# Expert results of a gated transformer block: scattered to DRAM by token instead of stored by sorted tile and gathered

## The reference

```
logits = x_flat @ Wr                       # 2048 x 8
w, ind = top_k(logits, 2); w = softmax(w)
for each expert e:                         # hidden 1024 in layer 1, 512 in layer 2
    y_e = gelu(x_flat @ W1e + b1e) @ W2e + b2e
    acc += combine[:, e] * y_e             # combine is zero for an expert the token does not use
x = x + tanh(g) * acc                      # layer 2 adds its own normalised input as well
```

## Time and profile before

| | us |
|---|---|
| median of three runs | 1596.48 |
| span of the profiled execution, first to last instruction | 1607.0 |
| PE / DVE / ACT / POOL busy in the span | 1331.3 / 965.3 / 864.4 / 706.4 |
| last matmul of the last tile, layer 1 | ends at 818.3 |
| first attention matmul of layer 2 (L940) | 898.97 |
| last matmul of the last tile, layer 2 | ends at 1252.0 |
| first attention matmul of layer 3 | 1330.62 |

### The profile page before, as it was taken

How to read it: one execution, slowest core, us unless ns; L and a number is a source line. 1 busy time by engine, 2 the same in 40 slices (tenths; PEclk the granted TensorE clock), 3 DMA queues, 4 the chain that set the end, 5 groups by cost and what they waited for, 6 DMA issues and landing times.

```text
span 1607.0 us, 29299 instructions
## 1 busy us (share of the span) xinstructions
PE 1331.3 (83%) x9524; PEld 954.1 (59%) x9524; DVE 965.3 (60%) x2636; ACT 864.4 (54%) x1718; POOL 706.4 (44%) x823
## 2 busy tenths in 40 slices
PE   1699899987987499999986699838989767995985
PEld 1355489754655399999963456527868434555433
DVE  6779653427866633333345588574535467867787
ACT  2356854335885255555523388535545245885564
POOL 4557330125623477676045473157772536623000
PEclk9989999997999699999998699968999987997998
DMA  9989030279921334633145985024643479920001
GB/s 286 294 128 143 4 115 1 82 215 173 131 37 60 123 93 140 200 143 109 46 138 170 209 122 82 2 89 146 202 154 113 149 216 177 129 43 1 0 14 40
DMA packets 144175, 189.63 MB, mean 118 GB/s; under 512 B 21936, under 2 KB 110384, under 8 KB 143984
## 3 DMA queue, kind: packets, MB, share of 16 engines
q0 software_dynamic: 79264, 103.35, 32.7%
q1 hardware_dynamic: 64768, 84.41, 16.3%
HBM read 128.96 MB, written 50.99 MB: 112 GB/s over the span
## 4 chain that ended last, share of the span: by engine, by line
PE 51%; DVE 14%; POOL 11%; DMA 10%; issue 6%; ACT 6%; another core or an unknown queue 1%; SPq 0%; DVEq 0%; POOLq 0%; ACTq 0%
PE PS L1176 8%; PE PS L1156 8%; PE PS L997 6%; PE PS L940 5%; DMA stack<-mt 3%; PE PS L967 3%; DVE nm L2052 2%; PE PS L1034 2%; PE PS L1168 2%; DMA qk_parts<-q_parts 2%; POOL weights L747 2%; DMA wslot<-ys_sorted,pos 2%; POOL weights L742 1%; PE PS L977 1%
## 5 line engine op out<-in xcount | busy, mean ns | idle before, releaser
L2052 DVE TENSOR_REDUCE nm<-PS 128x2 f32<-128x512 f32 x384 | 251.7, 680 | 50.4 <-PE PS L940 50.3
L1176 PE MATMUL PS<-weights,hh 128*128 x936 | 188.9, 291 | 3.2 <-DVE hl L2365 3.2
L1156 PE MATMUL PS<-weights,xh 128*128 x468 | 171.6, 422 | 10.2 <-DVE xl L2349 4.6
L940 PE MATMUL PS<-stack 48*128 48x256 f32 x1024 | 142.1, 359 | 41.6 <-DVE nm L2052 12.9
L645 POOL DMA_DIRECT2D stack<-mt x128 | 71.5, 559 | 223.7 <-ACT mt L1485 220.8
L1476 ACT ACTIVATE probs<-PS 128x512 f32<-128x512 f32 x256 | 138.9, 595 | 45.7 <-PE PS L967 22.3
L940 PEld LDWEIGHTS PS<-stack 48*128 48x128 f32 x1024 | 85.6, 206 | 125.8 <-issue 65.0
L1476 ACT ACTIVATE xng<-PS 128x512 f32<-128x512 f32 x256 | 138.9, 594 | 39.8 <-PE PS L977 21.6
L1176 PEld LDWEIGHTS PS<-weights,hh 128*128 128x128 f32 x936 | 152.0, 192 | 4.6 <-issue 4.3
L1643 ACT ACTIVATE hh<-PS 128x512 fp32r<-128x512 f32 x117 | 65.6, 596 | 131.2 <-PE PS L1168 127.9
L1176 PE MATMUL PS<-weights,hl 128*128 x468 | 132.7, 284 | 0.0
(11 more groups left out here) (321 smaller groups left out, 3102.4 us busy)
## 6 DMA issues: line engine op xcount, KB each, us to landing
stack<-qk_parts POOLq DMA_DIRECT2D x128, 256.0 KB, 4.1
qk_parts<-stack SPq DMA_DIRECT2D x32, 512.0 KB
qk_parts<-q_parts SPq DMA_DIRECT2D x32, 512.0 KB, 8.0
stack<-qk_parts POOLq DMA_DIRECT2D x128, 128.0 KB, 3.7
weights<-W_dram POOLq DMA_DIRECT2D x12, 1024.0 KB, 8.1
ys_sorted<-yo SPq DMA_DIRECT2D x78, 128.0 KB
wide<-ctxT_dram SPq DMA_DIRECT2D x16, 512.0 KB, 5.9
weights<-W_dram POOLq DMA_DIRECT2D x12, 512.0 KB, 5.3
```

Of the source, the lines that this page charges most:

```text
L940: mm = pe.matmul(PS[:, (2 * t + h) % 3, qt * S:(qt + 1) * S], q[rows, qt * P:(qt + 1) * P], kk[rows], start=True, stop=True)
L1156: add = lambda x, w: pe.matmul(PS[:, hid_bank(p) + h, :], x[:, p, c, :], w, start=False, stop=True, skip_group_check=True)
L1176: add = lambda x, w: pe.matmul(o, x, w, start=False, stop=True, skip_group_check=True)
L2052: nc.vector.tensor_reduce(nm[:, j % 2, at:at + 2], PS[:, (2 * t + h) % 3, :].rearrange("p (q n) -> p q n", q=2), AX.X, ALU.max, negate=Tru ...
```

## The change

Results stay in SBUF: `result(i)` is the place in `wide` (i < 16) or the `home` of tile i, which the gathered tile has left by then. POOL, after its last weight split, issues 39 indirect scatters, tile by tile, each behind `yo_done` of that tile, to a DRAM tensor `yt` laid out by expert choice and token; padding rows go to rows of their own at its end. The index table `into` is made in `plan` beside `idx`, by six DVE operations where two stood (`rows_of_tiles`, called for 8 and for 31 tiles). SP loses its 39 stores; after the last `load_tile` it loads the projections, then the context once the first 16 scatters have landed, then, once all have, the results by eight plain loads of 512 KB. DVE adds four blocks for one choice, four for the other, then does four statistics.

```diff
+        def result(i):
+            return wide[:, i * D:(i + 1) * D] if i < 2 * AHEAD else home(i)
...
-        ys = nc.dram_tensor("ys_sorted", (NT * P, D), F32, kind="Internal").ap()
+        yt = nc.dram_tensor("y_tokens", (P + 2 * T + NT * P, D), F32, kind="Internal").ap()
...  # SP
-                sp.wait_ge(y_done[2], 24)
+                sp.wait_ge(y_done[2], 16)
...
-                    sp.dma_start(ys[2 * T:], io["ctx"][0:NT * P - 2 * T, :]).then_inc(later_in, 16)
+                    sp.dma_start(xt[0:P], io["ctx"][0:P, :]).then_inc(later_in, 16)
...
-                    def store_tile(i, p):
-                        sp.wait_ge(yo_done, n0 + i + 1)
-                        sp.dma_start(ys[P * i:P * (i + 1), :], yo[:, p]).then_inc(ys_out[p], 16)
-                    for i in range(AHEAD - 3):
-                        store_tile(i, i % 2)
                     for i in range(AHEAD, NT):
...
                         load_tile(i, i % 2)
-                        if 0 <= i - 2 * AHEAD - 2 < GROUPS:
-                            load_ctx(i - 2 * AHEAD - 2)
-                        store_tile(i - 3, (i - 3) % 2)
                     load_proj(l + 1)
-                    for i in range(NT - 3, NT):
-                        store_tile(i, i % 2)
+                    sp.wait_ge(yt_out[0], 16 * l * 2 * AHEAD)
+                    for g in range(GROUPS):
+                        load_ctx(g)
+                    sp.wait_ge(yt_out[1], 16 * l * (NT - 2 * AHEAD))
+                    for g in range(GROUPS):
+                        for m in range(2):
+                            first = P + m * T + g * 512
+                            sp.dma_start(yg[:, m * TILES + 4 * g:m * TILES + 4 * g + 4, :],
+                                         yt[first:first + 512, :].rearrange("(t p) d -> p t d", p=P)).then_inc(yg_in[2 * g + m], 16)
...  # POOL
-                    pool.wait_ge(placed, l)
-                    for p in range(2):
-                        pool.wait_ge(ys_out[p], 16 * ((NT + 1 - p) // 2) * l)
-                    for k in range(FED[l]):
-                        if k >= 8:
-                            pool.wait_ge(y_done[l], added(k - 8))
-                        nc.gpsimd.indirect_dma_start(yg[:, k, :], None, ys,
-                                                     bass.IndirectOffsetOnAxis(pos[:, k % 2, k // 2:k // 2 + 1], 0)
-                                                     ).then_inc(yg_in[k % 8], 16)
+                    pool.wait_ge(placed, 2 * l)
+                    for i in range(NT):
+                        pool.wait_ge(yo_done, NT * (l - 1) + i + 1)
+                        nc.gpsimd.indirect_dma_start(yt, bass.IndirectOffsetOnAxis(into[:, i:i + 1], 0), result(i), None
+                                                     ).then_inc(yt_out[i // (2 * AHEAD) > 0], 16)
...  # PE
-                pe.wait_ge(idx_done, 2 * l)
+                pe.wait_ge(placed, 2 * l)
...  # DVE
+            def rows_of_tiles(l, k, first, part, block):
+                n = part.shape[1]
+                at = slice(first, first + n)
+                tmp = lambda r: scan[:, 0].rearrange("p t e -> p (t e)")[:, 32 * (r + 1):32 * (r + 1) + n]
+                ts, tt = nc.vector.tensor_scalar, nc.vector.tensor_tensor
+                ts(tmp(0), block, TILES + 0.5, -float(T), ALU.is_gt, ALU.mult).then_inc(route_v[l], 1)
+                dve.wait_ge(route_v[l], k + 1)
+                tt(tmp(1), part, tmp(0), ALU.add).then_inc(route_v[l], 1)
+                dve.wait_ge(route_v[l], k + 2)
+                nc.vector.scalar_tensor_tensor(idx[:, at], block, float(P), tmp(1), ALU.mult, ALU.add).then_inc(idx_done, 1)
+                nc.vector.scalar_tensor_tensor(tmp(2), block, 0.5, pad_row[:, at], ALU.is_lt, ALU.mult).then_inc(route_v[l], 1)
+                dve.wait_ge(route_v[l], k + 3)
+                tt(tmp(0), part, tmp(2), ALU.add).then_inc(route_v[l], 1)
+                dve.wait_ge(route_v[l], k + 4)
+                nc.vector.scalar_tensor_tensor(into[:, at], block, float(P), tmp(0), ALU.mult, ALU.add).then_inc(placed, 1)
+                return k + 4
...
-                nc.vector.tensor_copy(pos[:], posf[:]).then_inc(placed, 1)
...
-                    nc.vector.tensor_copy(yo[:, p], PS[:, 5, 0:D]).then_inc(yo_done, 1)
+                    nc.vector.tensor_copy(result(i), PS[:, 5, 0:D]).then_inc(yo_done, 1)
...
+                for g in range(GROUPS):
+                    for m in range(2):
+                        dve.wait_ge(yg_in[2 * g + m], 16 * l)
+                        for t in range(4):
+                            at = 4 * g + t
+                            if m:
+                                dve.wait_ge(y_done[l], 8 * g + t + 1)
+                            nc.vector.scalar_tensor_tensor(x_res[:, at, :], yg[:, m * TILES + at, :], gt[:, 6 + m, at:at + 1],
+                                                           x_res[:, at, :], ALU.mult, ALU.add).then_inc(y_done[l], 1)
+                    for t in range(4):
+                        dve.wait_ge(y_done[l], 8 * g + t + 5)
+                        stats(2 * l + 2, 4 * g + t)
+                    group_variances(2 * l + 2, g)
```

More of the change, by code:

```diff
@@ L68 @@
 ROUTE = 17
-PLANNED = 56
+PLANNED = 59
 BY_GROUP = (0, 4, 6)
@@ L226, in build @@
         idx = sb("idx", [P, NT], U32, fs)
+        into = sb("into", [P, NT], U32, fs)
         late = sb("late", [P, NT - 4 * AHEAD, D], F32, fs)
@@ L297, in ctx_at @@
             return xnT[:, :, g * 512:(g + 1) * 512]
-        xt = nc.dram_tensor("x_tokens", (T, D), F32, kind="Internal").ap()
-        ys = nc.dram_tensor("ys_sorted", (NT * P, D), F32, kind="Internal").ap()
+        xt = nc.dram_tensor("x_tokens", (P + T, D), F32, kind="Internal").ap()
+        yt = nc.dram_tensor("y_tokens", (P + 2 * T + NT * P, D), F32, kind="Internal").ap()
         parts = nc.dram_tensor("qk_parts", (2, 2, 2 * DH, PAIRS, T), F32, kind="Internal").ap()
@@ L2238, in plan @@
                     dve.wait_ge(later_in, 64)
+                    ts(pad_row[:], iotas[:, 2 * TILES + 1:2 * TILES + 1 + NT], float(P), col("part"), ALU.mult, ALU.add)
                 for m in range(2):
@@ L2294, in plan @@
                 dve.wait_ge(idx_mm, 2 * l - 1)
-                then(nc.vector.tensor_copy(late[:, 0, 0:AHEAD], PS[:, 6, 0:AHEAD]))
-                nc.vector.scalar_tensor_tensor(idx[:, 0:AHEAD], PS[:, 6, AHEAD:2 * AHEAD], float(P), late[:, 0, 0:AHEAD],
-                                               ALU.mult, ALU.add).then_inc(idx_done, 1)
+                k = rows_of_tiles(l, k, 0, PS[:, 6, 0:AHEAD], PS[:, 6, AHEAD:2 * AHEAD])
                 for e in range(8):
@@ L2329, in plan_late @@
                     ins = tt(ids_late[:, at, rest:], ids_late[:, at, 0:rest],
-                             iotas[:, 0:TILES].unsqueeze(2).broadcast_to([P, TILES, rest]), ALU.mult)
+                             iotas[:, 1 + m * TILES:1 + (m + 1) * TILES].unsqueeze(2).broadcast_to([P, TILES, rest]), ALU.mult)
                 then(ins)
@@ L2333, in plan_late @@
                 dve.wait_ge(idx_mm, 2 * l)
-                then(nc.vector.tensor_copy(late[:, 0, 0:rest], PS[:, 7, 0:rest]))
-                nc.vector.scalar_tensor_tensor(idx[:, AHEAD:], PS[:, 7, rest:2 * rest], float(P), late[:, 0, 0:rest],
-                                               ALU.mult, ALU.add).then_inc(idx_done, 1)
+                rows_of_tiles(l, k, AHEAD, PS[:, 7, 0:rest], PS[:, 7, rest:2 * rest])
             def sparse(l):
@@ L2367, in d, with e @@
                                                 ).then_inc(hl_done, 1)
-                def e(i, p, turn):
+                def e(i):
                     dve.wait_ge(tiles_done, t0 + i + 1)
-                    before = ((NT + 1) // 2 if p == 0 else NT // 2) * (l - 1) + turn - 1
-                    if not (isinstance(turn, int) and before == 0):
-                        dve.wait_ge(ys_out[p], 16 * before)
-                    nc.vector.tensor_copy(yo[:, p], PS[:, 5, 0:D]).then_inc(yo_done, 1)
+                    nc.vector.tensor_copy(result(i), PS[:, 5, 0:D]).then_inc(yo_done, 1)
                 dve.wait_ge(tables, l)
@@ L2395, in sparse @@
                     dve.wait_ge(ln_x, 1)
[L2396 to L2401, removed]
-                        nc.vector.scalar_tensor_tensor(x_res[:, at, :], yg[:, k, :], gt[:, 6 + n // 2, at:at + 1], x_res[:, at, :],
-                                                       ALU.mult, ALU.add).then_inc(y_done[l], 1)
-                    if t % 4:
-                        g = t // 4
-                        stats(2 * l + 2, t - 2)
-                        stats(2 * l + 2, t - 1)
-                        dve.wait_ge(y_done[l], 2 * t + 4)
-                        stats(2 * l + 2, t)
-                        stats(2 * l + 2, t + 1)
-                        group_variances(2 * l + 2, g)
-                        if g + 1 < GROUPS:
-                            keys_low(l + 1, g + 1)
-                        else:
```

(9 more changed lines are left out.)

13 lines of the change are left out of this document (5 added, 8 removed).

## The result

Before and after were timed in turn on one chip: 1641.59 us after (median of 4 runs, 1640.85 to 1645.09) against 1597.53 us before (1594.42 to 1599.38). The ratio is 1.026, with a 95% interval of 1.022 to 1.030. **The change makes the kernel 44 us slower; 7 us faster was forecast, and the time lies above the range.** The profiled execution has a span of 1639.0 us against 1607.0, with PE busy 1334.7 us at a mean clock of 0.916.

What follows compares the result with a forecast made beforehand. PE bounds layer 1's tiles; the winnable part lies between tiles and attention. Loads -14.2 and -2.6, plan +2.0 give -14.8; plus 8 for hand-offs absent in the runs, -7: 1596.48 to 1589 us, range 1579 to 1604.

Steps and rivals of the forecast that it cites:

- Tile loop: Both layers' tiles: stores leave SP, scatters go to idle POOL; caught up by about 802, 17 us late in layer 2.
- rival C: Layer 2's scatters cost more than gathers, 1.6 us each, ending 13.7 us later: 1603 us; chance 0.20.
- turns of layer 1 grow beyond 6.73 us while scatters run: Sign against the forecast: PE's tiles in layer 1, following at 6.73 us, slow down beside POOL's scatters.
- Scatter price, 1.25 us: POOL's scatters behind its last split: each taken to cost 1.25 us, like gathers in a run.
- Late hand-offs "absent in the runs": DVE and ACT waits after indirect DMA runs, 18 us in the profile: 10.5 us of them taken as absent when timed.
- The 10.5 us between its profile and its median: Profiled span 1607.0 us against run median 1596.48: the profiled execution held at least 10.5 us that the runs don't.
- Loads, layer 1: Between tiles and attention, eight plain loads replace gathers: low part of first queries at 860.5, 14.2 us earlier.
- 828.3 + 32 + 2 = 862.3: Layer 1 terms: first load there at 828.3, four groups of work 32 us, 2 us lost to a late key store.
- Loads, layer 2: Between tiles and attention, plain loads wait for the last scatter: low part of first queries at 1310.5, 2.6 us earlier.
- Plan, +2.0 us: Index plan, both layers: more small DVE operations delay first gather and second tile, +1.0 us a layer; bounds 0 and +4.
- The 8 us taken off: Share of the 14 us of late hand-offs between tiles and attention assumed absent in the runs, so not winnable.
- POOL's tail of 17 us: Layer 2: 39 scatters at 1.253 us from 1220.1 end at 1269.0, 17 us after the last tile.

Runs made afterwards that it cites:

- e1: The changed kernel without any scatter, its eight loads reading x_tokens instead: 1587.34 us, ratio 0.991 to the kernel before.
- e3: The changed kernel with each scatter replaced by a plain DMA of the same tile from the same queue: 1570.63 us, ratio 0.980 to the kernel before.
- e4: The kernel before plus 30 unneeded back-to-back scatters behind POOL's last weight split in each layer: 1663.83 us, ratio 1.044 to the kernel before.
- e5: The changed kernel with each scatter turned into a gather of 128 rows from x_tokens: 1654.32 us, ratio 1.035 to the kernel before.
- e8: The changed kernel with scatters of 64 rows in place of 128: 1644.43 us, ratio 1.029 to the kernel before.
- e11: The kernel before with a 128x1 GpSimd addition behind each of its back-to-back gathers: 1609.67 us, ratio 1.005 to the kernel before.
- e12: The changed kernel with 128x1 additions behind scatters and back-to-back gathers, and three scatters behind each weight load of experts 3 to 7: 1596.63 us, ratio 1.001.
- e9: The changed kernel with a 128x1 GpSimd addition behind each scatter: 1583.71 us, ratio 1.000 to the kernel before.
- e15: The changed kernel with a 128x1 addition behind each scatter, timed again on another chip: 1631.58 us, ratio 1.021 to the kernel before.
- e13: The changed kernel with a 128x256 GpSimd addition behind each scatter: 1604.47 us, ratio 1.003 to the kernel before.
- e14: The changed kernel, three scatters behind weight loads of experts 3 to 7, two inside splits of 6 and 7, 128x256 additions between the last 20: 1576.54 us, ratio 0.988.
- e6: The changed kernel with a 128x512 GpSimd addition behind each scatter: 1633.66 us, ratio 1.022 to the kernel before.
- e10: The changed kernel with scatter i waiting until i - 2 has landed and context loads waiting for all scatters: 1612.50 us, ratio 1.019.
- e2: The changed kernel with scatters spread: four behind each load of weights, two inside each of the last three splits, rest at the end: 1586.68 us, ratio 0.990.

## Why the prediction was wrong

**The step that failed** is in "Tile loop": the scatters "are POOL's, behind the last split, where it was idle", and then only POOL's own time was counted. I asked who waits for the scatters and not what they do to hand-offs beside them. The cost was 30.6 and 36.2 us: without the scatters it is gone (e1), with plain DMAs too (e3), and the kernel before gets it from 30 scatters alone (e4). I had seen the effect around the gathers and wrote under rival C that 39 indirect DMAs "could do the same to hand-offs" and that in layer 1 nothing covers it, but I gave it no price. The rows held a hint and no bound: 4 to 8 us of late hand-offs behind runs of 8 to 24, in places where few hand-offs were due. In the tile loop they are few, too, but far longer: in layer 1 three steps of the chain, of 21.3, 9.2 and 4.0 us. The loss comes near the length of the whole run: 31 to 42 us in each layer of the changed kernel, e4, e5 and e8, whose runs last 34 to 40 us. Why it is so much more than behind the gathers is not shown. The condition "I am wrong if turns of layer 1 grow beyond 6.73 us while scatters run" is what came true.

**Scatter price, 1.25 us: right.** 1.27 in a run (0.96 and 0.30 idle), as the gathers (the longest gather of a tile takes 1.91 us, not 1.88, but nothing rests on it). Rival C's price of 1.6 us is refuted, though its side was right.

**Late hand-offs "absent in the runs": not so for those of the tiles.** The runs have them as the profile has: +44 us against +32 in the spans, and +63 in e4. The few of the kernel before stay undecided (e11). The 10.5 us between its profile and its median, on which the forecast took 8 us off, prove nothing: beside e11 and e12, 22 executions of the kernel before lie between 1589.16 and 1610.11 us.

**Loads, layer 1: 14.2 us forecast, 18.4 measured.** The first adds come at 859.28, 7 us behind the last tile, not 9 to 10. The key store does land late (issued at 865.61; ACT waits 4.19 us for it at 873.87; 2 were assumed). The forecast's own terms do not quite give its times: 828.3 + 32 + 2 = 862.3 and 1277.5 + 32 = 1309.5, 12.4 and 3.6 us earlier where it wrote 14.2 and 2.6. The Trainium skill ("DMA: Bandwidth & Descriptors", Issuing engines are not separate DMA queues) says that the transfers of SP and POOL run on the same DMA engines and interleave. That did not decide anything here: e3 moves the bytes of the scatters from the same queue and stalls nothing.

**Loads, layer 2: 2.6 us forecast, 23.6 measured** (1252.01 to 1313.08 against 1301.87 to 1339.36), but for a reason without merit. The stalled tiles gave POOL time to catch up, so its last scatter went out at 1302.57, 0.7 us behind the start of the last result's copy. Where nothing stalls the forecast holds: in e9 the last scatter leaves 19 us behind the last tile and the tail is 4.6 us shorter than before (74.5 against 79.1).

**Plan, +2.0 us: too much.** From the last product of `eq` to the first indices is 8.3 us before and 8.4 after in layer 2, the first gather comes 0.1 us later behind it, and from the first indices to the late ones it is 14.7 and 14.3. Of layer 1's 3.1 us 2.8 come before the plan.

**The forecast without its gap.** e3, which differs from the changed kernel only in the kind of DMA, has 0.980 (-32 us): the forecast of -7 was too small for the case without the stall. The 8 us taken off and POOL's tail of 17 us, which plain DMAs of 0.54 us don't have, would make up the difference, but that is a sum and not an experiment; e1, which issues nothing, has 0.991.

## What to carry to other kernels

Idle time of GpSimd is not free room for indirect DMAs: a run of them stops engines that have nothing to do with them, so put them in ones to threes between its other work, or pace them, here at 1.8 us or more. When a profile shows "remote" waits that end behind such a run, price that effect in any stretch to which a change moves the run: between the waits seen and, where PE hands over all the time, the length of the whole run. Where the order of the rows allows it, plain DMAs from the same queue are twice as quick to issue and did none of this.

## What the runs showed of the hardware

Indirect DMAs issued by GpSimd every 1.20 to 1.27 us, some 30 in a row, hold up hand-offs from PE to ACT and DVE by up to 35 us at a time (e5); gathers and scatters alike, with 128 or 64 rows. At 1.37 us it came in two of three cases (up to 28.6 us between results in e15, 11.9 in e12, nothing in e9). At 1.80 us (e13, e14, timed with e15) and at 2.2 us (e6, timed with e5 and e8, which stall) it did not come; twos at a mean of 1.7 to 1.8 us (e10) had none either, but were timed only with e9. Four in a row with a gap behind them held up a result by 3.2 to 4.0 us in four of layer 1's five groups (e2), three in a row by at most 0.3 us (e14). Plain DMAs 0.54 us apart do nothing of the kind. A scatter of 64 rows takes 0.89 us of issue, one of 128 rows 0.96. What inside GpSimd or behind it holds the hand-offs was not found: the profile names nothing, and the DMA engines were at 0.29 of their time. One rival is open. The trace loses records just there: of the 16 semaphore increments due between 760 and 798 us it has 7, of the 156 between 700 and 755 all. Every execution here, the timed ones too, has its span and granted clock on record, so no run tells whether a kernel that nothing records would stall as well.
